# A perceiver block on one core: another order for the first batch pair of its cross-attention

## What is computed

```python
x = x + _L0_xattn_ref(_layernorm(x), ctx_1024, ctx_1024, mask, Wq, bq, Wk, bk, Wv, bv, Wo, bo)
# inside: 16 heads of 32 features
Q = query @ Wq.T + bq; K = key @ Wk.T + bk; V = value @ Wv.T + bv
weights = softmax(where(mask == 0, -inf, Q K^T / sqrt(32)))
attn = (weights @ V) @ Wo.T + bo
```

## Time and profile before

| | us |
|---|---|
| median of 3 runs (lowest, highest) | 809.27 (809.18, 809.61) |
| the profiled execution | 809.27 |
| its span | 807.3 |
| PE busy in the span | 775.0 |
| DVE busy | 624.6 |
| ACT busy | 471.0 |
| POOL busy | 242.6 |

### The profile page before, as it was taken

One profiled execution on the slowest core, in us unless ns is written; L12 is line 12 of the kernel. 1 busy time (PEld: TensorE's weight loads), 2 busy tenths in 40 slices (PEclk: granted clock), 3 DMA queues, 4 the chain that ended last, 5 costly groups with the idle time before them and its releaser, 6 DMA issues.

```text
span 807.3 us, 22183 instructions
## 1 busy us (share of the span) xinstructions
PE 775.0 (96%) x8851; PEld 460.1 (57%) x8851; DVE 624.6 (77%) x990; ACT 471.0 (58%) x847; POOL 242.6 (30%) x413
## 2 busy tenths in 40 slices
PE   8989999999999999999999999995999999999995
PEld 3445545555445555455557544554967866876783
DVE  4977888879788888787768668788778788778860
ACT  4546666656665565665547133238568758857960
POOL 0235234433354433344430200012153241331220
PEclk9999999999999999999999999996999999999998
DMA  8324453344413345323523511104899988998500
GB/s 306 140 64 109 106 155 94 80 107 108 94 41 93 94 107 134 64 71 106 122 55 57 209 53 53 53 0 137 287 386 415 405 348 290 350 350 301 230 31 15
DMA packets 94901, 125.56 MB, mean 156 GB/s; under 512 B 76352, under 2 KB 79168, under 8 KB 83956
## 3 DMA queue, kind: packets, MB, share of 16 engines
q1 hardware_dynamic: 92260, 117.65, 45.6%
q0 software_dynamic: 2576, 7.02, 2.4%
HBM read 100.47 MB, written 6.88 MB: 133 GB/s over the span
## 4 chain that ended last, share of the span: by engine, by line
PE 81%; DVE 11%; ACT 3%; DMA 2%; issue 1%; POOL 1%; SPq 1%; POOLq 0%; DVEq 0%; ACTq 0%
PE bank L1474 60%; PE bank L1852 10%; PE bank L1643 4%; DVE arena L933 3%; PE bank L1824 3%; PE bank L1609 3%; ACT arena L695 2%; DVE arena L989 1%; DMA arena<-arena 1%; DMA arena<-in_wv_t 1%; DVE arena L995 1%; ACT arena L662 1%; PE bank L1811 1%; DVE arena L948 1%; DVE arena L965 1%
## 5 line engine op out<-in xcount | busy, mean ns | idle before, releaser
L1474 PE MATMUL bank<-arena 128*128 128x160 f16 (+8 forms) x3944 | 562.9, 303 | 8.2 <-DVE arena L1366 2.0
L1474 PEld LDWEIGHTS bank<-arena 128*128 128x128 f16 (+2 forms) x3944 | 322.4, 100 | 236.6 <-issue 13.8
L662 ACT ACTIVATE arena<-arena 128x256 f16<-128x256 f32 (+5 forms) x302 | 254.1, 889 | 21.8 <-PE bank L1824 7.9
L933 DVE SCALAR_TENSOR_TENSOR arena<-arena 128x2048 f16<-128x2048 f32 (+4 forms) x102 | 200.5, 1987 | 37.5 <-ACT arena L662 34.6
L662 ACT ACTIVATE arena<-bank 128x512 f16<-128x512 f32 x175 | 100.1, 584 | 144.4 <-PE bank L1474 110.6
L933 DVE SCALAR_TENSOR_TENSOR arena<-bank,arena 128x512 f16<-128x512 f32 x174 | 116.8, 682 | 44.4 <-ACT arena L662 40.8
L1852 PE MATMUL bank<-arena 128*128 128x512 f16 x384 | 86.6, 379 | 0.0
L695 ACT ACTIVATE arena<-arena 128x257 f32<-128x257 f32 x128 | 63.5, 498 | 21.9 <-DVE arena L997 21.9
L528 POOL TENSOR_TENSOR arena<-arena 32x1024 f16<-32x1024 f32 (+1 forms) x16 | 34.1, 2132 | 140.1 <-PE bank L1643 139.9
L1852 PEld LDWEIGHTS bank<-arena 128*128 128x128 f16 x384 | 36.1, 98 | 41.1
L545 POOL COPY arena<-arena 32x256 f16 (+1 forms) x128 | 50.3, 393 | 24.0 <-DVE arena L933 11.8
(11 more groups left out here) (112 smaller groups left out, 486.1 us busy)
## 6 DMA issues: line engine op xcount, KB each, us to landing
arena<-in_w SPq DMA_DIRECT2D x64, 1024.0 KB, 6.8
arena<-in_ctx_t SPq DMA_DIRECT2D x15, 1024.0 KB, 5.4
arena<-in_awt SPq DMA_DIRECT2D x3, 1024.0 KB, 7.1
l_dram<-arena SPq DMA_DIRECT2D x4, 512.0 KB, 4.4
x_dram<-arena SPq DMA_DIRECT2D x1, 2048.0 KB, 13.7
arena<-in_wk_t SPq DMA_DIRECT2D x4, 256.0 KB, 4.8
arena<-in_ctx_t SPq DMA_DIRECT2D x4, 256.0 KB, 6.8
arena<-in_wv_t SPq DMA_DIRECT2D x1, 1024.0 KB, 8.2
```

Source lines behind the costliest of these rows:

```text
L662: return a.activation(dst, src, ACT.Copy, scale=scale)
L933: return v.scalar_tensor_tensor(dst, src, scale, h, ALU.mult, ALU.subtract)
L1474: last = m.matmul(out_ap, w, x, start=(n == 0), stop=(n == len(pairs) - 1))
```

## The change

It moves and swaps work of step 0 and of the start of step 1; no matmul, activation or element operation is added or dropped. In the order of the program:

- PE: the first value products wait for both halves of Wv (`w_lo`) ahead of the first one, where they waited for the lo half only before their last four matmuls. The first two query products use BA and BB (before: BA and BD). The last products come after query 2 and ahead of the second half's transposes; they use BD and BC (before: BC and BD), and a wait for `q_f32` ahead of their second part is gone. Queries 4 and 5 both come before `scores(0, 0)`, query 6 between the two batches' scores, query 7 behind them.
- POOL: both `power` steps come ahead of the first `query_hi`; the last `query_hi` comes ahead of `last_keys(0, 1)`.
- ACT: bv's row is written before the queries, the last products before the second transposes; `p_hi(0, 1)` moves behind `query(7)`, to the start of step 1.
- DVE: the lo part of the second context tile comes ahead of `normalise(1)`, bv's row and the last products ahead of `query_lo(1)`; in step 0 `reciprocals(0, 0)` and `query_lo(5)` come ahead of the second batch's scores, and `p_lo(0, 1)` moves behind `k_lo(0)` of step 1.
- SP: the second mixing weight is loaded right behind the first, for which the fp32 query buffers move into the unused part of pT; the second DMA transpose of step 0 therefore waits until all queries are split. bv's staging row moves.

```diff
         FIRST_PROJ = (BA, BB, BE, BC, BD, BA, BB, BC)
-        Q_BANKS = (BA, BD, BB, BA, BB, BA, BB, BG)
+        Q_BANKS = (BA, BB, BA, BB, BA, BB, BA, BG)
         FOLD_BANKS = (BC, BA, BD, BB)
...
         mask_int = view(sm_off, [L], I32)
+        q_f = [view(pt_off + P_BLOCKS * P * 2 + n * 2 * KB, [D], F32) for n in range(2)]
         vlast = [view(sm_off + 2 * KB + n * 256, [P], F16) for n in range(2)]
-        bv_stage = view(pt_off, [KC, P], F32)
+        bv_stage = view(sm_off + 2 * KB + 512, [KC, P], F32)
...
         xhat0 = view(wt_off, [NT, D], F32)
-        q_f = [view(wt_off + 4 * W_HALF + n * 2 * KB, [D], F32) for n in range(2)]
...
             load_mixing(0)
+            load_mixing(1)
...
                 for b in range(PB):
+                    if m == 0 and b == 1:
+                        sp.wait_ge(s["q_lo"], 2 * KC)
                     sp.wait_ge(s["p_lo"], m * 8 + (4 + 4 * b))
...
                 if m == 1:
-                    sp.wait_ge(s["q_lo"], 2 * KC)
-                    load_mixing(1)
+                    sp.wait_ge(s["q_ps"], 2 * KC)
                     load_mixing(2)
...
             pool.wait_ge(s["chain_pool"], 1)
+            power(0)
+            power(1)
...
-            power(0)
-            query_hi(0)
-            power(1)
-            for n in range(1, KC):
+            for n in range(KC):
                 query_hi(n)
...
             last_keys(0, 0)
-            last_keys(0, 1)
             query_hi(KC + 3)
+            last_keys(0, 1)
             queries_of(1)
...
                 hi(ctx_hl[1][0], ctx_stage[1], SX).then_inc(s["split_hi"], 1)
+                act.wait_ge(s["last_zero"], 1)
+                act.wait_ge(s["consts_landed"], 16 * (7 + HC))
+                for rows in (B, 2 * B):
+                    hi(vl_cur[rows:rows + 1].rearrange("p (b c) x -> p b c x", b=PB),
+                       bv_stage[rows:rows + 1].unsqueeze(1).broadcast_to((1, PB, KC, P)), SX).then_inc(s["bv_hi"], 1)
                 act.wait_ge(s["bq_done"], 1)
...
                 query(2)
-                tokens_hi(lnT_tile, 0, 1)
-                query(3)
                 act.wait_ge(s["last_ps"], 1)
-                hi(vlast[0], BC[:, 0:P], 1.0 / SW).then_inc(s["last_hi"], 1)
+                hi(vlast[0], BD[:, 0:P], 1.0 / SW).then_inc(s["last_hi"], 1)
                 act.wait_ge(s["last_ps"], 2)
-                hi(klast[0], BD[:, 0:KC * B].rearrange("p (c b) -> p c b", c=KC), SK / (SX * SW)
-                   ).then_inc(s["last_hi"], 1)
-                act.wait_ge(s["last_zero"], 1)
-                act.wait_ge(s["consts_landed"], 16 * (7 + HC))
-                for rows in (B, 2 * B):
-                    hi(vl_cur[rows:rows + 1].rearrange("p (b c) x -> p b c x", b=PB),
-                       bv_stage[rows:rows + 1].unsqueeze(1).broadcast_to((1, PB, KC, P)), SX).then_inc(s["bv_hi"], 1)
+                hi(klast[0], BC[:, 0:KC * B].rearrange("p (c b) -> p c b", c=KC), SK / (SX * SW)).then_inc(s["last_hi"], 1)
+                tokens_hi(lnT_tile, 0, 1)
+                query(3)
                 query(4)
...
                 exp(0, 1)
-                p_hi(0, 1)
                 query(7)
...
-                if st > 1:
-                    p_hi(st - 1, 1)
+                p_hi(st - 1, 1)
                 k_hi(0)
...
                 query_lo(0)
-                normalise(1, xhat0)
                 dve.wait_ge(s["split_hi"], 2)
                 lo(ctx_hl[1][1], ctx_stage[1], SX, ctx_hl[1][0]).then_inc(s["split_lo"], 1)
-                query_lo(1)
-                tokens_lo(lnT_tile, 0, range(HT, HT + 2))
-                query_lo(2)
-                tokens_lo(lnT_tile, 0, range(HT + 2, NT))
-                query_lo(3)
+                normalise(1, xhat0)
+                dve.wait_ge(s["bv_hi"], 2)
+                rows = slice(2 * B, 2 * B + 1)
+                own = vl_cur[rows].rearrange("p (b c) x -> p b c x", b=PB)
+                lo(own, bv_stage[rows].unsqueeze(1).broadcast_to((1, PB, KC, P)), SX, own).then_inc(s["bv_lo"], 1)
                 dve.wait_ge(s["last_hi"], 1)
-                lo(vlast[1], BC[:, 0:P], 1.0 / SW, vlast[0]).then_inc(s["last_lo"], 1)
+                lo(vlast[1], BD[:, 0:P], 1.0 / SW, vlast[0]).then_inc(s["last_lo"], 1)
                 dve.wait_ge(s["last_hi"], 2)
-                lo(klast[1], BD[:, 0:KC * B].rearrange("p (c b) -> p c b", c=KC), SK / (SX * SW), klast[0]
+                lo(klast[1], BC[:, 0:KC * B].rearrange("p (c b) -> p c b", c=KC), SK / (SX * SW), klast[0]
                    ).then_inc(s["last_lo"], 1)
+                query_lo(1)
+                tokens_lo(lnT_tile, 0, range(HT, NT))
+                query_lo(2)
                 dve.wait_ge(s["ab_split"], 2)
                 lo(ab[1], ab_sd, SW, ab[0]).then_inc(s["ab_split"], 1)
-                dve.wait_ge(s["bv_hi"], 2)
-                rows = slice(2 * B, 2 * B + 1)
-                own = vl_cur[rows].rearrange("p (b c) x -> p b c x", b=PB)
-                lo(own, bv_stage[rows].unsqueeze(1).broadcast_to((1, PB, KC, P)), SX, own).then_inc(s["bv_lo"], 1)
+                query_lo(3)
                 dve.wait_ge(s["vlast_stored"], 2 * KC * 16)
...
                 query_lo(4)
+                reciprocals(0, 0)
+                query_lo(5)
                 for j in range(KC, PAIRS):
...
                 maxima(0, 1)
-                reciprocals(0, 0)
-                query_lo(5)
+                query_lo(6)
                 p_lo(0, 0)
                 reciprocals(0, 1)
-                query_lo(6)
-                p_lo(0, 1)
                 query_lo(7)
...
                 k_lo(0)
-                if cur and st > 1:
+                if cur:
                     p_lo(st - 1, 1)
...
                 pe.wait_ge(s["proj_free"], (0, 1, 2, 4)[t])
-                if t == 0:
-                    pe.wait_ge(s["w_hi"], 1)
-                for u, z in ((0, 0), (1, 0), (0, 1)):
-                    if t == 0 and z == 1:
-                        pe.wait_ge(s["w_lo"], 1)
-                    for k in range(KC):
-                        last = m.matmul(FIRST_PROJ[KC + t][:], ctx_hl[0][u][:, k, t * P:(t + 1) * P], wv[z][:, k, :],
-                                        start=(k == 0 and u + z == 0), stop=(k == KC - 1 and z == 1))
-                last.then_inc(s["proj_ps"], 1)
+                product(FIRST_PROJ[KC + t][:], [(ctx_hl[0][u][:, k, t * P:(t + 1) * P], wv[z][:, k, :])
+                                                for k in range(KC) for u, z in ((0, 0), (0, 1), (1, 0))]
+                        ).then_inc(s["proj_ps"], 1)
...
             first_keys()
+            pe.wait_ge(s["w_lo"], 1)
             for t in range(3):
...
             for n in range(2):
-                pe.wait_ge(s["proj_free"], 6 - n)
+                pe.wait_ge(s["proj_free"], 6 + n)
                 for k in range(KC):
...
                 last.then_inc(s["q_ps"], 1)
-            pe.wait_ge(s["proj_free"], 7)
             queries(range(2, 3))
-            transpose_tokens(0, xhat0, 1)
-            queries(range(3, KC))
...
                     for c in range(KC):
-                        last = m.matmul(BC[c * B:(c + 1) * B, 0:P], ctxl[u][:, k, :], wv[z][:, k, c * P:(c + 1) * P],
+                        last = m.matmul(BD[c * B:(c + 1) * B, 0:P], ctxl[u][:, k, :], wv[z][:, k, c * P:(c + 1) * P],
                                         start=(k == 0 and u + z == 0), stop=(k == KC - 1 and u == 1))
             last.then_inc(s["last_ps"], 1)
-            pe.wait_ge(s["q_f32"], 2)
             for c in range(KC):
-                last = split_product(BD[:, c * B:(c + 1) * B], wk, ctxl,
+                last = split_product(BC[:, c * B:(c + 1) * B], wk, ctxl,
                                      lambda k: (slice(None), k, slice(c * P, (c + 1) * P)),
...
             last.then_inc(s["last_ps"], 1)
+            transpose_tokens(0, xhat0, 1)
+            queries(range(3, KC))
             pe.wait_ge(s["tr_free"], NT)
-            queries(range(KC, KC + 1))
+            queries(range(KC, KC + 2))
...
             scores(0, 0)
-            queries(range(KC + 1, KC + 2))
+            queries(range(KC + 2, KC + 3))
             scores(0, 1)
-            queries(range(KC + 2, 2 * KC))
+            queries(range(KC + 3, 2 * KC))
             pe.wait_ge(s["q_f32"], 2 * KC - 1)
```

16 lines of the change are left out of this document (8 added, 8 removed).

## The result

The changed kernel took 815.21 us (median of 4 executions, 815.08 to 815.38), the kernel before 809.22 beside it: ratio 1.0081, 95% interval 1.0067 to 1.0095. It is slower by 6.0 us. The forecast was 812.7, its range ended at 814.6: the direction was right, the size too small by 2.5 us.

The account below looks back on a forecast made before the run. PE was taken as the bound, busy 775.0 of 807.3 us, so only its idle time and low clock could pay. 2.3 us won against 3.9 of new waits gave 809.27 + 1.6 + 1.8 = 812.7 us, range 809.8 to 814.6.

Parts of the forecast that it names:

- BB: PE's first queries in step 0: query 1 waits 1.7 us until DVE has read BB's value product, before 0.31.
- second normalisation: Before PE's second transposes in step 0: a wait of 0.35 us for DVE's tiles, transposes starting at 42.55.
- the tokens' lo parts: Before query 4 in step 0: PE waits 1.4 us for DVE's lo parts of the transposed tiles, ready at 48.3.
- The chain of batch 1's weights: Step 0 scores to step 1 attention: DMA transpose lands at 75.7, PE is there at 73.1 and waits 2.6 us.
- the landing of the DMA transpose: Batch 1's weights, end of step 0: 4.4 us from issue at 71.3 to landing at 75.7.
- The contention: `p_lo(0, 1)` on DVE beside POOL's spreading of step 1's queries: taken as 1.8 us, with 0.64 kept for the range.
- take turns: Rival, chance 0.03: each of `p_lo(0, 1)`'s four operations waits out a POOL operation of 0.6 us; +2.4 more, 815.1 us.
- The price of the clock: Behind the 2.6 us wait in step 1: PE's clock falls to 0.50 and costs 1.78 us, from between 0 and 1.78.
- Clock holds: Rival, chance 0.16: the long wait in step 1 has no clock fall behind it; +1.6, 810.9 us.
- a second fall: Rival, chance 0.09: the clock also falls behind the 1.7 or the 1.4 us wait; +1.78 more, 814.5 us.
- No bound: Rival, chance 0.06: batch 1's weights chain does not bound, landing before 71.8; step 1's gain of 2.3 stays, 806.9 us.
- DVE's order: Step 0 softmax: batch 1's additions queue behind batch 0's reciprocals and `query_lo(5)`, from 57.8 to 60.55; 2.7 us of the chain.

Follow-up runs that it names:

- second profile: The changed kernel measured once more, unedited ("again"), against the kernel before: 811.14 us against 803.53, ratio 1.0097; its profiled execution took 811.96 us.
- first profile: The changed kernel as first measured, unedited: its profiled execution took 810.39 us, where the median of its executions was 815.21.
- the third: The changed kernel measured a third time, unedited, against the kernel before: 811.55 us against 804.34, ratio 1.0089.
- the deferral without collisions: Kernel before with batch 1's step 0 weights deferred, POOL's step 1 queries behind the last lo weight, six start fillers made 64 small products: 804.12 us against 804.34.
- the second group: Kernels measured together on one chip, among them the unchanged kernel before against itself: 804.88 us against 803.59, ratio 1.0012.
- the first and last groups: Two sets of kernels measured together, each with the unedited changed kernel against the kernel before: 811.14 against 803.53 us and 811.55 against 804.34.
- the version with step 1 written out: Changed kernel with 18 unused products of 512 columns on PE between step 1's two attentions: 809.82 us against 803.53 for the kernel before, ratio 1.0086.

## Why the prediction was too low

**What held.** The waits of the prologue came as forecast, in both profiles of the changed kernel (first, again): value products 0.44 forecast, 0.52 and 0.33; BB 1.7, 1.59 and 1.68; second normalisation 0.35, 0.29 and 0.29; the tokens' lo parts 1.4, 1.52 and 1.51. `queries_of(0)` was hidden and the clock of 53 to 54 us was 1.00. The chain of batch 1's weights was named as the bound, and released the long wait.

**What held by luck.** The first key product of step 1 was forecast at 60.4 and began at 60.48 and 61.05. But the forecast let the value products begin at 18.21, and they began at 17.49 and 18.06. From there to the first key product it laid out 42.2 us; both profiles took 43.0. The same goes for the issue of the transpose, forecast and found at 71.3: in the second profile it came at 71.9, and counted from the value products it was 0.7 us late in both.

**The step that failed: the end of the chain of batch 1's weights, and above all the landing of the DMA transpose.** The last lo half and the transpose were priced at 1.8 + 4.4 = 6.2 us and took 2.43 + 5.5 = 7.9. For the landing the prediction took 4.4 us from the earlier trace rows, the minimum and the median. The row's maximum, 6.2, was there, and neither priced nor put into the range. It measured 5.5, and the runs show why: a fetch of PE's program falls into the transfer. So the wait was 4.16 instead of 2.6; 1.1 us of that is the landing, and the rest is that the wait before the fourth key product came to 0.55 instead of 1.3 (PE was there sooner and stood longer). Together 4.7 against 3.9.

**The contention was under-sized.** `p_lo(0, 1)` was put at 1.8 us and took 2.43, at the upper end of what the prediction kept for the range. The early start of the first profile hid this error in the time of issue; the chain from the first scores to `p_lo(0, 1)` took 15.6 us where 15.9 were laid out. The prediction saw its rule for two SBUF inputs confirmed by the 0.64 us that `normalise` lost beside POOL's casts; those tiles are `TENSOR_SCALAR` operations with one input tile, so they don't test it. The rival "take turns" named the right mechanism with the wrong unit: 0.77 us in all (2.43 less 1.66), not 2.4.

**The price of the clock.** 1.78 us was taken from one fall. The low clock behind the 4 us wait cost, in attention, scores and two value products, 1.4 us in the first profile, 2.8 in the second and 1.2 in the third (7.07 us at full speed; 77.41 to 87.27 in the second profile, 76.90 to 85.35 in the first). It is a spread and not a number. The fall behind the kernel before's 2.08 us wait, which the change removes, is itself not certain: in the profile of the deferral without collisions the same wait stands with query 5 at 2.76 us behind it, not 4.45 (so the fall costs 1.7 there). The sum credited its full 1.78 to the change. In the three groups where the kernel before took some 804 us its executions spread from 802.2 to 806.6, as such a fall that comes and goes would make them. Their mean granted clocks agree: in the second group the nine executions at 0.984 and less took 803.6 to 805.9 us, nine of the ten at 0.985 and 0.986 took 802.2 to 803.3. The four executions of the changed kernel in each of the first and last groups all lie at 0.981 or 0.982. That the fall is the whole of the spread is argued.

**What was left out.** Products take 2.69 us between scores, not 2.61, and PE pauses 0.27 us ahead of step 1's first key product, where its loop over the steps begins; no releaser stands for it. The kernel before and the version with step 1 written out have no such pause, and what makes it is open. From the first scores to the first key product this makes 0.5 us. And the sum of before's waits missed two, of 0.19 at 40.45 and of 0.47 at 46.71; since the forecast laid out positions and not differences, it changed nothing.

**Added up.** In the second profile, where PE reaches the value products at 17.73 (before 17.77), the second scores of step 1 start at 87.27, against 81.12 before: 6.15 us late. The forecast had 3.4. The waits of step 1 are 0.75 more, the clock 1.0, the start of the key products 0.65 and the rest of step 1 at full speed 0.3: 2.7. Counted in the same way, from where PE reaches the value products, the first profile is 5.0 us late and the third 4.8, with the clock 0.4 and 0.6 under its 1.78: the excess that all three share is 1.8 to 2.1 us, and the clock is not in it. The measured loss was 6.0 us at first, 7.6 and 7.2 later. That the later ones are over 6 would follow from the executions of the kernel before whose clock held; that is argued.

**The rivals.** "Clock holds" and "a second fall" didn't come. "No bound" didn't either: the chain was the bound, and even with the weights back in step 0, where PE waits only 0.56 us for the landing but 1.89 before the fourth key product, the time was 3.2 us above the kernel before. The attribution inside the chain was wrong in one place: it gave 2.7 us to DVE's order, which by experiment is worth 0.7 at most, and nothing to the deferral apart from its queue positions, which is worth 4 to 5 us. In the kernel before all of that comes through the two collisions and the wait's own fall of the clock. In the changed kernel, where PE is sooner at the attention, a wait of 2.33 us is left without them, and the time stays 0.7% above the kernel before.

## What to carry to other kernels

An operation that is deferred must be priced at its new place with what runs beside it there, and up to the landing of the transfer that hangs on it: in the kernel before the same deferral cost 4.9 us with a POOL operation and a program fetch in its way and nothing without them. Where a chain ends in a DMA whose minimum and maximum differ, put the maximum into the range and look for what was in the record when it was late; here the trace of the kernel before had the packet at its latest landing. When an order on the critical engine looks right but loses, try its feeders' orders first; here that took a loss of 0.9% back to nothing. And a fall of the clock that comes and goes is credited to a change only in part: the same code had it in some executions and not in others.

## What the runs showed of the hardware

- A packet of PE's instruction queue (0.02 MB) that falls into SBUF-to-SBUF DMA transposes holds them up by about 1.0 to 1.7 us: batch 1's landed after 5.4 to 6.2 instead of 4.4 to 4.5 us in step 0, and of all 544 none landed after more than 4.7 us without a packet of an instruction queue in it. Shifting PE's program by some 116 instructions moved it away, and in one kernel into the other batch's transposes, which then took 5.6.
- POOL and DVE hold each other up by whole instructions where both work on SBUF: a POOL copy of 0.21 us took 2.28 beside a DVE operation of 2.42, two POOL products of together 1.18 took 3.55 beside 3.83 us of DVE, four DVE operations of 1.66 took 2.43.
- TensorE's granted clock fell to 0.50 behind a wait of 2.15 us in one of two profiles with the same code up to there, and behind the 2.08 us wait of the kernel before in three of four profiles (the fourth with other fillers at the start). It held behind one of 2.33. In all eight profiles with a wait of 3.1 us or more there it fell, and cost from 1.1 to 2.8 us.
- Stops of some 0.4 us without a releaser in the experts, with cycles longer by 4 to 7 us in all, were there in all four profiles of one group and in none of an earlier one on the same chip. What makes them is open.
